# Reciprocal softmax sums turned by transfers, pair by pair, in a two-layer transformer block

## What is computed

```python
def attention0(x, w_qkv, w_out):        # 8 heads of 64, windows of 128 rows and both neighbours
    q = k = rotary(x @ w_qkv[:512].T);  v = x @ w_qkv[512:].T
    sim = where(mask, -max, q @ k.T)
    return (softmax(sim) @ v) @ w_out.T
def ffn0(x):                            # 8 experts and a shared one, 2 of 8 by the router
    probs = softmax(x @ router_w + router_b)
    top, idx = top_k(probs, 2)
    return shared(x) + sum(weight[e] * (gelu(x @ rw1[e] + rb1[e]) @ rw2[e] + rb2[e]))
x = L0_attn_x;      xn = layernorm(x)
x = x + attention0(layernorm_gb(xn)) + ffn0(xn)
xn = layernorm(x)
x = x + gated_attention1(layernorm_gb(xn)) + ffn1(xn)   # 32 experts, 8 of 32
```

## Time and profile before

| | us |
|---|---|
| median of 3 runs | 1018.01 |
| lowest and highest | 1014.0, 1018.76 |
| the profiled execution | 1016.07 |
| its span, first to last instruction | 1014.8 |
| TensorE busy | 970.2 |
| VectorE busy | 674.2 |
| ScalarE busy | 513.8 |
| GpSimd busy | 434.2 |

### The profile page before, as it was taken

How to read it: one execution, slowest core, us unless ns; L and a number is a source line. 1 busy time by engine, 2 the same in 40 slices (tenths; PEclk the granted TensorE clock), 3 DMA queues, 4 the chain that set the end, 5 groups by cost and what they waited for, 6 DMA issues and landing times.

```text
span 1014.8 us, 13581 instructions
## 1 busy us (share of the span) xinstructions
PE 970.2 (96%) x4532; PEld 635.2 (63%) x4532; DVE 674.2 (66%) x1571; ACT 513.8 (51%) x1202; POOL 434.2 (43%) x343
## 2 busy tenths in 40 slices
PE   5998889999999999999999999999999999999998
PEld 3664556676665766667665766657666576657655
DVE  5945858777674876658766587666787477625933
ACT  3663674454745357462663627545375445635222
POOL 5856325752074510945027530465206542045333
PEclk9999999999999999999999999999999999999999
DMA  7050340520433115230142301532024220343061
GB/s 272 22 158 0 33 125 1 114 67 11 85 87 93 43 12 124 67 92 23 12 138 70 81 17 12 149 85 72 0 44 138 71 54 11 85 106 87 19 156 34
DMA packets 63237, 72.80 MB, mean 72 GB/s; under 512 B 33272, under 2 KB 34040, under 8 KB 62784
## 3 DMA queue, kind: packets, MB, share of 16 engines
q1 hardware_dynamic: 61744, 69.94, 27.7%
q10 hardware_dynamic: 1424, 2.00, 0.6%
HBM read 69.04 MB, written 2.88 MB: 71 GB/s over the span
## 4 chain that ended last, share of the span: by engine, by line
PE 66%; POOL 12%; DMA 9%; DVE 8%; issue 2%; ACT 2%; SPq 0%; DVEq 0%; ACTq 0%; POOLq 0%
PE ps L725 11%; PE ps L476 7%; PE ps L478 6%; PE ps L477 6%; PE ps L530 6%; PE ps L555 6%; PE ps L543 6%; POOL pt L1837 5%; DMA wide<-scratch 5%; DMA scratch<-pt 3%; POOL atc L1833 3%; PE ps L618 3%; PE ps L700 2%; POOL kr L1825 2%; POOL qr L1827 2%
## 5 line engine op out<-in xcount | busy, mean ns | idle before, releaser
L1128 ACT ACTIVATE wide<-ps 128x512 f32<-128x512 f32 x136 | 81.0, 596 | 219.7 <-PE ps L478 219.1
L1057 ACT ACTIVATE pw<-ps,w_cols 128x512 f32<-128x512 f32 x144 | 98.6, 687 | 104.5 <-PE ps L478 102.4
L1017 ACT ACTIVATE pw<-ps,nmax 128x256 f32<-128x256 f32 x256 | 118.8, 476 | 56.8 <-DVE nmax L1376 56.7
L618 PE MATMUL ps<-pw,w_w 128*128 128x512 f32 x288 | 137.7, 601 | 1.5 <-DVE pt L1453 1.5
L1843 POOL TENSOR_TENSOR atc<-atc,wide 128x512 f32<-128x512 f32 x64 | 82.3, 1286 | 126.2 <-DVE atc L1582 126.2
L1825 POOL TENSOR_TENSOR kr<-qks,w_rope 128x512 f32<-128x512 f32 x32 | 42.4, 1324 | 167.6 <-DVE qks L1354 167.6
L1387 DVE COPY pt<-ps 128x512 f32<-128x512 f32 x128 | 83.0, 683 | 30.8 <-PE ps L543 30.6
L476 PE MATMUL ps<-yc,eg 128*128 128x512 f32 x128 | 94.3, 737 | 0.0
L1376 DVE TENSOR_REDUCE nmax<-ps 128x4 f32<-128x1024 f32 (+1 forms) x80 | 79.1, 1005 | 19.5 <-PE ps L530 19.5
L1843 POOL TENSOR_TENSOR pt<-pt,wide 128x512 f32<-128x512 f32 x48 | 61.7, 1286 | 63.0 <-DVE pt L1582 61.9
L476 PE MATMUL ps<-yc,w 128*128 128x512 f32 x144 | 80.9, 562 | 2.4 <-ACT pw L1057 2.4
(11 more groups left out here) (223 smaller groups left out, 2130.6 us busy)
## 6 DMA issues: line engine op xcount, KB each, us to landing
wb<-scratch SPq DMA_DIRECT2D x128, 256.0 KB, 4.0
wb<-scratch SPq DMA_DIRECT2D x32, 512.0 KB, 6.4
wide<-scratch SPq DMA_DIRECT2D x16, 512.0 KB, 6.1
xin<-in_x SPq DMA_DIRECT2D x8, 256.0 KB, 3.1
out<-wide SPq DMA_DIRECT2D x8, 256.0 KB, 2.1
wb<-in_w SPq DMA_DIRECT2D x1, 1152.0 KB, 8.7
w_w<-in_w SPq DMA_DIRECT2D x1, 1152.0 KB, 11.9
w_ed<-in_ed SPq DMA_DIRECT2D x1, 1024.0 KB, 16.4
```

What stands on the lines that cost most here:

```text
L618: pe.matmul(bank(k), w2[:, e, c, :], hid[:, n % 4, :], start=c == 0, stop=c == 1 and e < E0).then_inc(*DOWN0.one)
L1017: m = act.activation(pw[:, u % 2, j, :], ps[:, score_bank(u, par), qt * SEQ:(qt + 1) * SEQ], ACT.Exp, bias=nmax[:, u % 3, j:j + 1], scale= ...
L1057: act.activation(hid[:, n % 4, :], bank(UPS0[n % 2]), ACT.Gelu, bias=cols[:, C_B1 + 2 * e + c:C_B1 + 2 * e + c + 1], scale=1.0).then_inc(* ...
```

## The change

- The 4 transposes of `rden`, ScalarE's copy and `wden` are gone. `denominators(s, p)` sends the 2 x 512 reciprocals of one pair of heads from rows to `scratch2`, each value of 4 bytes to its own place, waits for it, and loads `wide[:, p, :]` in two DMAs of 128 KB. There are four such turns in a step instead of one.
- SyncE's order for s>0: the weights' transfer, pairs 0 and 1, the `wb` loads, pairs 2 and 3. For s=0 all four stand where the one stood.
- GpSimd: for s>0 pairs 0 to 2 are normalised at the end of its `attention` program, ahead of what `experts0` begins with; pair 3 in `experts0`, ahead of the first `add0`.
- `out0` has two places, one of them `y0r` (`x1s` in step 0), and `weigh0(e)` waits for the `add0` of two experts before, no longer for the one just before.
- Logits in rows: the tokens' columns are the weights and the router's 16 (high and low) columns move, 8 short matmuls in place of 3 long ones and 4 turns. VectorE adds two parts and the bias. ScalarE's copy is gone.
- For s>1, `exp0` and `route0_weights` stand at the end of `experts1(s-1)` and no longer in unit 1.

```diff
-        rden = sb("rden", [P, TILES, HEADS])
+        rden = sb("rden", [P, HEADS, TILES])
-        wden = pt[0:HEADS, 0, 4:8, :].rearrange("p a q -> p (a q)")
-        out0 = pt[:, 0, 4:8, :].rearrange("p a q -> p (a q)")
+        out0 = [[(y0r if s else x1s)[:, :, :].rearrange("p t d -> p (t d)"),
+                 pt[:, 0, 4:8, :].rearrange("p a q -> p (a q)")] for s in range(STEPS)]
...
@@ SyncE
-            def denominators(s):
-                w.wait_ge(*DEN_COPIED.at(s))
-                w.wait_ge(*DEN_WIDE.at(s - 1))
-                sp.dma_start(scratch2, wden).then_inc(*SCRATCH2.one)
-                w.wait_ge(*SCRATCH2.at(s))
+            def denominators(s, p):
+                w.wait_ge(*INVERTED.at(s, G * p + G - 1))
+                w.wait_ge(*DEN_WIDE[p].at(s - 1))
+                by_token = bass.AP(tensor=scratch2.tensor, offset=2 * p * TOK, ap=[[1, P], [P, 2 * TILES]])
+                with nc.allow_non_contiguous_dma(reason="a sum of 4 bytes goes to each row"):
+                    sp.dma_start(by_token, rden[:, 2 * p:2 * p + 2, :].rearrange("p h t -> p (h t)")).then_inc(
+                        *SCRATCH2.one)
+                w.wait_ge(*SCRATCH2.at(s, p))
...
                 for par in range(2):
-                    src = bass.AP(tensor=scratch2.tensor, offset=par * TOK,
-                                  ap=[[0, 64], [2 * TOK, PAIRS], [1, TOK]])
-                    sp.dma_start(wide[64 * par:64 * par + 64, :, :], src).then_inc(*DEN_WIDE.one)
+                    src = bass.AP(tensor=scratch2.tensor, offset=(2 * p + par) * TOK, ap=[[0, 64], [1, TOK]])
+                    sp.dma_start(wide[64 * par:64 * par + 64, p, :], src).then_inc(*DEN_WIDE[p].one)
...
                     stage(8)
+                weights_layer0_rows(s)
+                if s:
+                    denominators(s, 0)
+                    denominators(s, 1)
                 weights_layer0(s)
                 if s == 0:
                     stage(5)
                     stage(6)
-                denominators(s)
+                    denominators(s, 0)
+                    denominators(s, 1)
+                denominators(s, 2)
+                denominators(s, 3)
...
@@ TensorE: turn_denominators and turn_logits0 are gone, with their calls and ScalarE's copies
             def logits0(s, k):
-                pe.matmul(wide, rw0[:, 0, :], columns0(s)[:, 0, :], start=True, stop=False)
-                pe.matmul(wide, rw0[:, 0, :], columns0(s)[:, 1, :], start=False, stop=False)
-                pe.matmul(wide, rw0[:, 1, :], columns0(s)[:, 0, :], start=False, stop=True).then_inc(*LOGITS0.one)
                 for t in range(TILES):
+                    c, rows = 2 * E0 * t, slice(t * P, (t + 1) * P)
+                    pe.matmul(bank(k)[:, c:c + 2 * E0], columns0(s)[:, 0, rows],
+                              rw0[:, :, :].rearrange("p a e -> p (a e)"), start=True, stop=False,
+                              skip_group_check=True)
+                    m = pe.matmul(bank(k)[:, c:c + E0], columns0(s)[:, 1, rows], rw0[:, 0, :],
+                                  start=False, stop=True, skip_group_check=True)
+                m.then_inc(*LOGITS0.one)
...
@@ ScalarE
-                    if u == 1 and not first:
+                    if u == 1 and second:
                         exp0(s)
...
                     exps(n, 0, 0)
+                    exp0(n)
                     exps(n, 0, 1)
...
@@ VectorE
             def weigh0(s, e):
                 if e == 0:
                     w.wait_ge(*WEIGHED.at(s))
                 else:
-                    w.wait_ge(*SCRATCH2.at(s))
-                    if e > 1:
-                        w.wait_ge(*ADDED0.at(s, e - 2))
+                    if e == 2 and s:
+                        w.wait_ge(*Y0_TURNED.at(s))
+                    if e > 2:
+                        w.wait_ge(*ADDED0.at(s, e - 3))
...
-                    if u == 1 and not first:
+                    if u == 1 and second:
                         route0_weights(s)
...
                     maxima(n, 1)
+                    route0_weights(n)
...
@@ GpSimd
             def attention(s):
...
+                if s:
+                    for p in range(PAIRS - 1):
+                        normalise(s, p)
...
             def experts0(s):
+                if s == 0:
+                    rope_turn(n, 0)
+                    add0(s, 1)
+                    rope_turn(n, 1)
+                    normalise(s, 0)
+                    add0(s, 2)
+                    rope_turn(n, 2)
+                    normalise(s, 1)
+                    add0(s, 3)
+                    rope_turn(n, 3)
+                    normalise(s, 2)
+                    add0(s, 4)
+                    normalise(s, 3)
+                    add0(s, 5)
+                    add0(s, 6)
+                    return
+                if more:
+                    rope_turn(n, 0)
+                    rope_turn(n, 1)
+                normalise(s, 3)
                 add0(s, 1)
                 if more:
-                    rope_turn(n, 1)
-                normalise(s, 1)
+                    rope_turn(n, 2)
                 add0(s, 2)
...
             def experts0_and_chain1(s):
                 rope1_turn(x, 1)
-                normalise(s, 0)
                 shortcut(x)
-                normalise(s, 1)
+                normalise(s, 3)
                 add0(s, 1)
```

More of the change, by code:

```diff
@@ L559, in weigh @@
                 freed[b] = OUT_COLS.at(s, u)
-            def turn_denominators(s, k):
-                w.wait_ge(*INVERTED.at(s))
-                take(k)
-                for t in range(TILES):
-                    m = pe.transpose(bank(k)[0:HEADS, t * P:(t + 1) * P], rden[:, t, :], ident[:, :])
-                m.then_inc(*DEN_TURNED.one)
-                freed[k] = DEN_COPIED.at(s)
             def logits0(s, k):
@@ L756, in attention @@
                         weigh(s, 0)
-                    if u == 0 and first:
-                        turn_logits0(0, score_bank(0, 1))
                     if u == 0 and second:
@@ L779, in attention @@
                 weigh(s, 7)
-                turn_denominators(s, 6)
                 if second:
@@ L827, in experts0 @@
                 if s == 0:
-                    turn_logits0(n, 6)
                     scores(n, 0)
@@ L890, in experts1 @@
                 uv(s, 2, 0, 3)
-                if more:
-                    turn_logits0(n, 2)
                 turn_y1(s, 6)
@@ L1237, in experts1 @@
                 silu(x, 3)
-                if more:
-                    logits0_copy(n, 2)
                 z1_cols(s, 6)
@@ L1410, in route0_logits @@
                 w.wait_ge(LOADED["rb0"], 16)
-                w.wait_ge(*LOGITS0_TURNED.at(s))
-                dve.tensor_tensor(lg0[:, :, :], bank(k)[:, 0:TILES * E0].rearrange(
-                    "p (t e) -> p t e", e=E0), spread(rb0[:, :], [(0, TILES), (1, E0)]),
-                    ALU.add).then_inc(*LOGITS0_ROWS.one)
+                w.wait_ge(*LOGITS0.at(s))
+                parts = bank(k)[:, 0:2 * TILES * E0].rearrange("p (t a e) -> p t a e", a=2, e=E0)
+                own(dve.tensor_tensor(lg0[:, :, :], parts[:, :, 0, :], spread(rb0[:, :], [(0, TILES), (1, E0)]),
+                                      ALU.add))
+                dve.tensor_tensor(lg0[:, :, :], parts[:, :, 1, :], lg0[:, :, :], ALU.add).then_inc(*LOGITS0_ROWS.one)
                 w.wait_ge(*LOGITS0_ROWS.at(s))
@@ L1467, in lay0 @@
                 w.wait_ge(*WEIGHTED0.at(s))
-                dve.tensor_tensor(lay[:, :], acc0, out0, ALU.add).then_inc(*LAY0.one)
+                dve.tensor_tensor(lay[:, :], acc0, out0[s][(E0 - 1) % 2], ALU.add).then_inc(*LAY0.one)
             def x1_rows(s, k):
@@ L1605, in attention @@
                     invert(s, u)
-                    if u == 0 and first:
-                        route0_logits(0, score_bank(0, 1))
                     if u == 0 and second:
@@ L1836, in add0 @@
                 w.wait_ge(*WEIGHTED0.at(s, e))
-                pool.tensor_tensor(acc0, acc0, out0, ALU.add).then_inc(*ADDED0.one)
+                if e > 1:
+                    w.wait_ge(*ADDED0.at(s, e - 2))
+                pool.tensor_tensor(acc0, acc0, out0[s][e % 2], ALU.add).then_inc(*ADDED0.one)
             def gate_hidden(s, c):
```

72 lines of the change are left out of this document (24 added, 48 removed).

## The result

| | before | changed |
|---|---|---|
| median of 4 runs | 1017.79 us | 1203.65 us |
| lowest and highest | 1014.0, 1018.76 | 1198.49, 1207.63 |
| profiled execution, its span | 1016.07, 1014.8 | 1198.49, 1197.2 |

The ratio is 1.183, with a 95% interval of 1.177 to 1.189: the change costs 186 us. Slower was forecast, 66 us of it.

The account below looks back on a forecast made before the run. TensorE, busy 96% of the span, was taken as the bound, GpSimd just behind in `experts0`. Terms 44 + 14 + 14 - 1 - 5 = +66 us on 1016.07 us gave 1082 us, range 1020 to 1130.

Parts of the forecast that it names:

- A pair's price: SyncE's transfer of a pair's 1024 reciprocals: 2 us plus 3.5 us for values at 3.5 ns each, 5.5 us in all.
- the quiet end: DMA engines quiet the last 8 us of the weights' wait: taken as a backlog of 4-byte writes, not a fixed receipt.
- Rival 2: Fixed quiet end of 8 us in each value-wise transfer: 12 us a pair standing alone, 1180 us and over; chance 8%.
- Pair 0 behind the weights: On SyncE, pair 0 queued behind the weights' transfer: back 3.5 us after the weights land, 510.3 to 513.8 in step 4.
- step 0: No scatter of weights, pairs known early; attention projection starts about 1 us later, the 3.9 us stall shrinks: -1 us.
- step 1: `rope1_turn` of layer 1, queued behind `normalise(1, 2)`, ends 15.2 us late, TensorE having about 1 us spare: 14 us.
- steps 2 to 6: In `experts0`, TensorE waits at the end of the chain pair 3, additions, last `weigh0`: 8.8 us a step, 44 us.
- step 7: No `rope_turn`; pair 3's late `wide` delays the first `add0`, so TensorE's bank for the sixth expert is late: 14 us.
- logits: Layer-1 experts: 8 short matmuls (0.96 us) replace `logits0` and `turn_logits0`, 0.7 us less TensorE a step, about 5 us.
- The moved `exp0` and `route0_weights`: Put before the attention's first copy of `pt` for s>1: costs nothing, or 0.5 us a step if cover is thin.
- Two places for `out0`: `weigh0(e)` runs without the add just before it, gaining a part of TensorE's 7.2 us of waits.
- Rival 1: A pair's values cost nothing, 2 us in all: -16 us, 1000 us; chance 8% for under 0.4 us.

Follow-up runs that it names:

- x2_eighth: Changed kernel sending only 128 of a pair's 1024 values, one per partition, to neighbouring places, `wide` loaded from an input: 1121.58 us.
- x3_spread: Changed kernel with a pair's 1024 values written 64 bytes apart, one to each 64 bytes, `wide` loaded from an input: 1029.63 us.
- x8_lone: Changed kernel with each of a pair's 1024 values alone in its own 512 bytes, `wide` loaded from an input: 1033.92 us.
- x7_apart: Changed kernel with a partition's eight values 8 bytes apart in one 64 bytes, partitions 512 bytes apart, `wide` loaded from an input: 1133.84 us.
- x1_block: Changed kernel with a pair's 1024 values written in 128 runs of 32 bytes, `wide` loaded from an input: 1009.67 us.
- x5_stride8: Changed kernel with a pair's 1024 values written 8 bytes apart, eight to each 64 bytes, `wide` loaded from an input: 1067.89 us.
- d3_rest: Kernel before with all of the change except the sums' way (sums still turned by TensorE and sent at the attention's end): 998.96 us, ratio 0.9825.
- d1_logits: Kernel before with only the layer-0 logits in rows and `exp0` and `route0_weights` moved ahead of the attention: 1000.13 us, ratio 0.9836.
- m1_moved: Kernel before with only `exp0` and `route0_weights` of steps 2 to 7 moved ahead of the attention: 1007.15 us, ratio 0.9929.
- d2_places: Kernel before with only the two places of `out0` for weighted outputs: 1007.48 us, ratio 0.9910.
- d4_pipe: Changed kernel with pairs 0 to 2 issued without waiting, then `wb` loads, pair 3, and only then the four waits with `wide` loads: 1108.68 us.

## Why the prediction was wrong, by its steps

**A pair's price: the step that failed.** "That leaves (16.4-2)/4096 = 3.5 ns a value, so 3.5 us more for a pair, 5.5 us in all." Measured 10.0 to 10.5, almost twice that; in its place x2_eighth and x3_spread show a price that goes by how many values share a place, and by their count far less than in proportion. Two readings went into it. One was the straight line through a single row: for this placing 128, 1024 and 4096 values take 6.7, 10.2 and about 16 us, so scaling down from the largest gives too little. The other was the choice about the quiet end in the earlier trace rows, "the quiet end is what a backlog of posted writes would leave as well, and a pair has a quarter of it". The trace after answers that. After pair 1 of step 4 the DMA engines stand still for 8 us, as long as after four times as many values:

```profile
606.00:608.00 2.00, 2.00 (x11) 1.49 (x11) 0.39 (x2) 1.79 (x4) 0.00 (x0) 1.00 0.74 114
608.00:616.00 8.00, 7.66 (x30) 4.71 (x28) 0.69 (x1) 4.42 (x7) 1.29 (x1) 1.00 0.00 0
```

Rival 2, with 12 us a pair and "1180 us and over", was the right one in size, and had 8%. As a mechanism it is only half right, since 1024 values with 64 bytes each have hardly any such end (x3_spread, x8_lone). The upper bound of 12 us held; the range of the whole time left it out, and that is where the range failed.

The Trainium skill, "DMA: Bandwidth & Descriptors", section "Specifications", says that below 512 bytes the DMA engine does a read-modify-write. That writes into the same 64 bytes then have to follow one another would fit the table above, but no run shows the writes themselves, x8_lone's single values are below that size too and cost 0.6 us more than runs of 32 bytes, and the 2.2 us of x7_apart aren't explained by it: argued, not shown.

**Pair 0 behind the weights.** Forecast 3.5 us after the weights' landing. A pair 0 took 21.0 us from its issue, in x1_block 14.7: 6.4 us more for how the values are written. The same mis-sizing.

**How the price reaches the end: near in size, only in part the path.** x5_stride8 has nearly the price that was forecast, 5.2 to 5.4 us a pair, and so tests the other steps (its `wide` loads read another place, with the same sizes). By stage, from its starts of L375 at 113.09, 259.01 and 902.02 and its span of 1066.6:

| | forecast | at the forecast's price (x5_stride8) | changed kernel |
|---|---|---|---|
| step 0 | -1 | -4.3 | +14.3 |
| step 1 | +14 | +9.6 | +20.6 |
| steps 2 to 6 | +44 | +35.1 | +116.9 |
| step 7 | +14 | +11.4 | +30.6 |
| logits | -5 | in the above | in the above |
| sum | +66 | +51.8 | +182.4 |

So the working gave 1082 where a kernel with such a price took 1068; the quiet parts, forecast at little more than the 5 us of the logits and worth 18 (d3_rest), are in that difference. The path in steps 2 to 6 was another than forecast. The forecast let TensorE wait at the end of the chain pair 3, additions, last `weigh0`, 8.8 us a step. At its own price TensorE waits for the turns behind pair 2, 7.1 us a step, and for `weigh0` only twice, 1.2 us in step 3 and 8.0 in step 7; x5_stride8's waits of TensorE:

```profile
PE ps L516 <- DVE qr L1350: 35.4, 5, 8.1
...
PE ps L621 <- DVE pt L1438: 9.1, 2, 8.0
```

In step 4 there, pair 3 is normalised at 566.73 us right behind the turns, with no wait. That the sizes agree, 8.8 and 7.1 us, is partly luck.

**Step 4 in the changed kernel.** Counted from the weights' issue (581.33 after, 493.8 in the forecast), pair 2 was normalised after 56.3 us in place of 47.4, and pair 3 after 68.3 in place of 55.2. TensorE's idle time in `experts0` grew by 18.7 us, not 8.8, to 20.5, nearly all of it in three places. The turns behind pair 2 hold TensorE for 8.9 us and the additions behind pair 3 for 2.9. The other 8.0 us are a term that the forecast put at nothing: "The first `weigh0` comes late too [...] but hides behind this." At the forecast's price it does hide (x5_stride8); at the real one `wb` comes too late, and 45.6 of TensorE's 75.4 us of waits for `weigh0` are these, one in each of steps 2 to 7. On top come 5.2 us that no step of the forecast had: the work behind the two long waits ran near the clock's lower level (0.57 and 0.51). The forecast read no row for what TensorE's clock does when TensorE waits; before, with 1.8 us of waits in this stretch, shows 1.00.

**Step 0.** The forecast took -1 us because its pairs "are known early". With 5.2 to 5.4 us a pair the pairs are covered: x5_stride8 has -4.3, and d3_rest, which sends the sums as before, -4.1. Four round trips of 8.8 to 13.0 us are no longer covered: TensorE waits 9.8 us for the last `normalise` there, one wait of L629.

**Steps 1 and 7.** In step 1 the mechanism was as described: TensorE waits for the rotary embedding of layer 1, 24.2 us in one wait, and 13.2 at the forecast's price (x5_stride8), where 14 was forecast. In step 7 it waits for `weigh0` twice, 16.6 us behind pair 3, as described and forecast at 14 (8.0 at the forecast's price), and 7.6 behind the late `wb`.

**The logits.** Forecast about 5 us from TensorE's pitch: 0.96 us for the new `logits0`. In d1_logits eight matmuls start within 0.69 us (seven distances), so some 0.8 us, and the net gain is 0.9 us a step. The whole of d1_logits gains 1.6%, some 16.5 us between the medians, and m1_moved alone 0.7%. Right in size for the matmuls, but the other gains were missed: 8.5 us are the move, and what the rest beyond the matmuls comes from was not taken apart.

**The moved `exp0` and `route0_weights`: wrong.** "Nothing, or 0.5 us a step if that cover is thin." The move gains 0.7%, 8.5 us between the medians. The 2.8 us that the weights' transfer gains were in the walk through step 4, but only as a part of the new chain; their worth in the old one, where it shortens what GpSimd and TensorE end on, wasn't counted.

**Two places for `out0`: right in kind**, "a part of the 7.2 us": 4.1 of them go. d2_places gains 0.9%, 9.1 us between the medians, more than that wait can give; where the other 5 come from is open.

**The rule that spoke against the change.** That a strided last dimension becomes one descriptor per element, quoted ahead, is borne out: 32 pairs of 1024 values and 7 transfers of 4096 weights make 61440 values, and the changed kernel has 67256 packets under 512 bytes. As a warning it pointed the right way, since a pair in runs of 32 bytes takes a quarter of the time. But x3_spread has the same 67256 packets and 3.1 to 3.3 us a pair: what costs is less their number than where they land. The fit of 2.0 us plus bytes over 436 GB/s stands in the Trainium skill ("DMA: Bandwidth & Descriptors", "Anatomy of one DMA") for transfers that GpSimd issues, and the forecast held it against SyncE's. By it a pair would have taken 2.0 us; that holds roughly for runs of 32 bytes (2.6) and is off by a factor of five for the values as they were written.

**Rival 1's sum** is written with its signs turned; its terms are -11 - 0.5 - 4 - 5 + 4 = -16.5, and the 1000 us stand.

## What to carry to other kernels

A scatter of single values is priced by where they land: before such a transfer is cut into smaller ones, measure one of the new size in the new placing, since a small one with the same neighbours keeps most of the large one's wait. A serial chain that crosses an engine's program several times in a step costs most of its length, and a third of the loss here was in what stood behind the waiting instruction; place the waiting instruction behind all that doesn't need it. And take a change of several parts apart: here three quiet parts were worth 1.8% and the fourth, the sums' way, cost more than ten times that.

## What the runs showed of the hardware that I had not expected

- 1024 writes of 4 bytes to DRAM take 3.1 to 3.3 us with each in its own 64 bytes and 10.0 to 10.5 us with 16 in 64 bytes; 128 of the latter take 6.7 us, more than 1024 of the former. Of the 11.4 us of such a pair in step 4, the DMA engines are shown standing still for 8.
- Eight values sharing 64 bytes are no cheaper if one partition sends all of them (6.3 to 6.4 us against 5.2 to 5.4), and dearer if such groups lie 512 bytes apart (8.4 to 8.6).
- Loads queued behind such writes without any wait between them land late: 512 KB in 14.9 us in place of 6.2 (d4_pipe).
- A stage in which TensorE waits 20.5 of 61.9 us ran at a granted clock of 0.86, and this alone was 5.2 of the 23.9 us that the stage lost. The clock was near its lower level (0.57 and 0.51) in the work right behind waits of 8.0 and 8.9 us, and 1.00 behind one of 2.9.
